# One activation table set, and the last row's inverse transform as four products without sums

## The reference

```python
x = x + attention(layernorm(x))               # 32 heads of 32, causal
x = x + autocorrelation(layernorm(x), ctx, ctx)
x = x + mix(layernorm(x))                     # four streams of 256
```

```python
corr = ifft(fft(q) * conj(fft(k))).real
w, idx = top_k(corr, 9); w = softmax(w)
out = sum_i w[i] * v[min(idx[i] + pos, L - 1)]
```

## Time and profile before

| what | value |
|---|---|
| median of 3 runs | 1248.21 us (1247.65 to 1251.31) |
| profiled execution, its own time | 1247.06 us |
| its span in the trace | 1245.1 us |
| PE busy | 1029.9 us, 83% |
| DVE busy | 932.4 us, 75% |
| ACT busy | 641.3 us, 52% |
| POOL busy | 492.4 us, 40% |

### The profile page before, as it was taken

The page is one execution under the profiler, slowest core; times in us unless marked ns, Lnnn a source line. Parts: engine busy times, 40 slices in busy tenths (PEclk is TensorE's granted clock), DMA queues, the critical chain, the costliest instruction groups (busy, mean ns, idle before and its releaser), DMA issues. The chain is left out here.

```text
span 1245.1 us, 23491 instructions
## 1 busy us (share of the span) xinstructions
PE 1029.9 (83%) x7928; PEld 781.0 (63%) x7928; DVE 932.4 (75%) x2818; ACT 641.3 (52%) x1827; POOL 492.4 (40%) x684
## 2 busy tenths in 40 slices
PE   5699999999999999999648999999887995615056
PEld 4577777787777777777436677767665663313034
DVE  6766787666678666666507778779998998897994
ACT  6434555544455544445516677778567655323133
POOL 2523443333343333344324666666565542201020
PEclk9799999999999999999679999999999997657578
DMA  9011011111101111110132123223222211139025
GB/s 377 25 42 57 19 57 57 57 57 40 45 28 57 57 57 57 40 41 19 58 120 85 68 83 117 89 77 123 73 81 81 73 39 38 43 120 332 0 56 131
DMA packets 47235, 95.72 MB, mean 77 GB/s; under 512 B 5952, under 2 KB 30400, under 8 KB 47168
## 3 DMA queue, kind: packets, MB, share of 16 engines
q1 hardware_dynamic: 47168, 94.91, 22.9%
HBM read 64.48 MB, written 27.26 MB: 74 GB/s over the span
## 5 line engine op out<-in xcount | busy, mean ns | idle before, releaser
L613 POOL TENSOR_TENSOR prob_G<-prob_G,rl 128x512 f32<-128x512 f32 x96 | 99.8, 1040 | 258.2 <-DVE rl L501 258.2
L383 ACT ACTIVATE prob_G<-prob_G,negm 128x128 f32<-128x128 f32 x384 | 148.8, 389 | 89.5 <-DVE negm L443 89.5
L244 PE MATMUL ps_qkv<-w_hi,xT_hi 128*128 128x512 f32 x384 | 156.7, 408 | 13.5 <-DVE prob_G L506 8.6
L245 PE MATMUL ps_qkv<-w_lo,xT_hi 128*128 128x512 f32 x384 | 151.4, 394 | 0.0
L246 PE MATMUL ps_qkv<-w_hi,xT_lo 128*128 128x512 f32 x384 | 151.2, 394 | 0.0
L316 PE MATMUL ps_qkv<-wo_hi,aT_hi 128*128 128x512 f32 x256 | 107.7, 421 | 0.0
L318 PE MATMUL ps_qkv<-wo_hi,aT_lo 128*128 128x512 f32 x256 | 102.1, 399 | 0.0
L317 PE MATMUL ps_qkv<-wo_lo,aT_hi 128*128 128x512 f32 x256 | 101.9, 398 | 0.0
L244 PEld LDWEIGHTS ps_qkv<-w_hi,xT_hi 128*128 128x128 f32 x384 | 73.2, 191 | 39.0 <-issue 16.1
L439 DVE TENSOR_TENSOR prob_G<-ps_s,mask 128x512 f32<-128x512 f32 x96 | 65.0, 677 | 41.4 <-PE ps_s L227 40.8
L468 DVE TENSOR_TENSOR xT_lo<-ps_t,xT_hi 128x512 fp32r<-128x512 f32 x16 | 11.1, 693 | 104.2 <-ACT xT_hi L422 104.2
(11 more groups left out here) (246 smaller groups left out, 2819.6 us busy)
## 6 DMA issues: line engine op xcount, KB each, us to landing
xin<-in_x SPq DMA_DIRECT2D x16, 512.0 KB, 3.3
xres<-in_x SPq DMA_DIRECT2D x16, 512.0 KB, 5.0
x<-xres SPq DMA_DIRECT2D x16, 512.0 KB, 2.6
c_xin<-x SPq DMA_DIRECT2D x16, 512.0 KB, 4.9
c_cin<-in_ctx SPq DMA_DIRECT2D x16, 512.0 KB, 4.2
c_b_xres<-x SPq DMA_DIRECT2D x16, 512.0 KB, 3.3
rows_x<-c_row SPq DMA_DIRECT2D x64, 128.0 KB, 2.3
m_xm<-rows_x SPq DMA_DIRECT2D x16, 512.0 KB, 8.6
```

What stands on the lines that cost most here:

```text
L244: nc.tensor.matmul(ps_qkv[:, n, :], xT_hi[:, k, :], w_hi[:, k, cols], start=k == 0, stop=False)
L245: nc.tensor.matmul(ps_qkv[:, n, :], xT_hi[:, k, :], w_lo[:, k, cols], start=False, stop=False)
L383: r = nc.scalar.activation(prob(g)[:, j, :], prob(g)[:, j, :], ACT.Exp, bias=negm[:, h:h + 1], accum_out=lsum[:, h:h + 1])
L613: nc.gpsimd.tensor_tensor(prob(g), prob(g), rl[:, g * GROUP:(g + 1) * GROUP].rearrange("p (j o) -> p j o", o=1).to_broadcast([P, GROUP, T] ...
```

## The change

Two edits. At ACT's start one set is named, which holds the logarithm beside the exponential and the copies, and is loaded there. In body 15 PE takes the four products themselves (the matrix that goes with each, `i % 2`, is that of the sum they belonged to), DVE makes the fourth with its sign turned, and POOL's sums of that body are gone. All bodies before it are as they were.

```diff
         @block.scalar
         def _(act):
+            nc.scalar.preload_act_table_set("natural_log_exp_and_others")
             act.wait_ge(const_in, 48)
...
                 def out_half(n):
+                    if not near:
+                        for i, part in enumerate((tw_re, tw_im, tw_re2, tw_im2)):
+                            if n == 0:
+                                pe.wait_ge(tw_done, 4 * b + (2, 2, 3, 4)[i])
+                            r = nc.tensor.matmul(p_b[:, n, :], mats[:, INV_OUT + i % 2, :], part[:, n * HALF:(n + 1) * HALF],
+                                                 start=i == 0, stop=i == 3)
+                        r.then_inc(out_ps, 1)
+                        return
...
-                        nc.vector.tensor_tensor(dst[:], src, of[:], ALU.mult).then_inc(tw_done, 1)
+                        if i == 3 and not near:
+                            nc.vector.scalar_tensor_tensor(dst[:], src, -1.0, of[:], ALU.mult, ALU.mult).then_inc(tw_done, 1)
+                        else:
+                            nc.vector.tensor_tensor(dst[:], src, of[:], ALU.mult).then_inc(tw_done, 1)
...
-                if far:
+                if far and near:
                     pool.wait_ge(tw_done, 4 * b + 3)
```

## The result

The changed kernel takes 1230.45 us, median of 4 runs (1229.03 to 1230.83). The kernel before took 1248.28 beside it, and the ratio is 0.985, 95% interval 0.9833 to 0.9868. Its profiled execution took 1230.26 with a span of 1228.4. The spans differ by 16.7; most of the rest of the 17.8 is that the execution profiled before was 1.2 faster than its own median, the changed one's only 0.2.

The account below looks back on a forecast made before the run. PE was taken as the bound up to body 7, DVE from body 8. Loads 8.9 plus body 15's 4.65 made 13.6 us: 1233.5 against the profiled 1247.06, 1234.6 for the median; range 1231 to 1242 for 8 in 10.

Parts of the forecast that it names:

- the term of 1.45: Body 6 into 7: without the load ahead of the exponential, the key spectrum PE waits for comes 1.45 us sooner.
- The first load of that turn: Body 6 into 7: this load delays only work that DVE doesn't yet need, so removing it gains 0.
- Start, 1.28: Kernel start: the load ahead of ACT's rounding of weights now runs while ACT waits for input, gaining 1.28 us.
- Body 11, body 14, body 17, the last exponential: Loads behind DVE's waits: body 11 gains 1.30 us, body 14 2.1, body 17 0.8, the end of mixing's chain_c 0.7.
- Body 15, 4.65: Body 15: DVE's 2.99 us wait for the second half goes, and 1.66 from chain steps slowed beside POOL's sums.
- The rival of the low clock: Body 15: PE's clock falls before the products, which take 1.91 us each; 6.2 us gained, 1242.0; 13%.
- The bounds of the fourth product: Body 15: the fourth product as scalar_tensor_tensor on DVE costs between 0 and +0.2 us more; 0 taken.
- The rule of half throughput: Body 15: by this rule the fourth product would take 1.1 us more, and the gain be 12.5 instead of 13.6.
- So all of it reaches the mixing phase: After body 15: bodies 16 and 17 take up none of the gain.
- Only the load at its end goes: 1.3: Mixing, chain_b: DVE's 9.1 us wait is mostly for rows read back; only its last load goes, 1.3 us.
- The drain: Rival at the loads: each also costs a drain, so 11 us more go and 1223.6 is left; 1%.
- two rivals: Low clock in body 15, 1242.0, 13%; gains before body 8 and in body 11 don't arrive, 1238.6, 17%.

Follow-up runs that it names:

- the set alone: The kernel before with only the one table set named at ACT's start, POOL's sums in body 15 kept: 1232.91 us.
- the products alone: The kernel before with only body 15's four products on PE without POOL's sums, all 25 loads kept: 1246.31 us.
- one moved line: chain_b's logarithms moved ahead of the take-outs of rows 0 and 1: on the changed kernel 1223.85 us; the same with POOL's sums in body 15 1230.24.

## Why the prediction was wrong

The direction, the places and most sizes held. The profiled execution was forecast at 1233.5 and took 1230.26: the sum failed by 3.2 us, of which the first point below is 1.8. The rest is the balance of small terms on both sides, some of them of single executions. Another 1.0 is the distance of the two profiled executions to their medians.

- **Body 6 into 7, the term of 1.45: the step that failed.** "PE stood idle 2.06 us for that spectrum. PE is the bound here: 1.45." The delay itself measured 1.62. But PE is the bound here, and its idle time was paid a second time in the work behind it, at half clock: 5.40 for the eight products instead of 3.70. The term measured 3.28. Both loads put back give exactly that, and with PE kept at work 1.85. I had the rule for body 15, where I priced the fall of the clock, and did not use it for the loads; the 5.40 stood in a row that I quoted.
- **The first load of that turn, priced at 0.** It holds back the squares, and so the second load. One load put back cost 0.79, both 3.28. They were one group, not one on the path and one hidden.
- **Start, 1.28.** It arrived (1.34 at DVE's first step behind it) and shrank to 0.5 by 820 in this trace. The low clock of 20.5 us near the end of the attention phase begins at 601.7 before and 601.5 after, so work that comes sooner can meet it at another place. How much is left is of the execution: -1.29 to +1.44 in twelve traces of the same program.
- **Body 11, body 14, body 17, the last exponential: 1.30, 2.1, 0.8, 0.7.** Measured 1.43, 2.26, 0.84 and 0.73. (Of the waits for the logarithms and exponentials there were seven and not six: DVE waits 0.5 for chain_c_logm too, before and after.)
- **959 to 1043 and the last rows, not priced: 1.09 and 0.73.** In the first the clock was low for 6.8 and 3.4 us before (ahead of the long low of body 14, which both have) and not at all after; in the last rows for 6.8 before and 3.4 after. The first can't be booked on the loads: the set alone gains 0.67 there, the products alone, with all their loads, 0.63, and both still have two low stretches of 3.4 us. So some 0.6 of the 1.09 is more likely what the profiled execution before had lost by itself. The second is firmer: of the eleven traces with the set named and nothing added at the last rows ten gain 0.73 to 0.87 there, and the products alone, with the load, gain 0.12; the pattern is that of body 7, and no experiment separates clock and load in it.
- **Body 15, 4.65.** Measured 4.77, and its two parts 3.05 and 1.72 where 2.99 and 1.66 were forecast. The rival of the low clock came in part: the clock fell after a wait of 1.23, and the slack of 1.4 took it up, with 0.56 of it left. The bounds of the fourth product, 0 to 0.2, held at 0. The rule of half throughput that I weighed against it (the Trainium skill, Vector Engine (DVE) Microarchitecture Reference, "7. Points that are easy to get wrong") is about two inputs in SBUF; this product has one of its two in the accumulators, so it doesn't test the rule: 1.22 either way. The row of 0.24 that has both the earlier trace rows is as fast as the plain form.
- **"So all of it reaches the mixing phase"** was right, and that the mixing phase would pass it on was not said but assumed. "Only the load at its end goes: 1.3" was 2.33 with the set alone and 0.32 with both. How long the wait is hangs on two rows' products, 1.97 or some 3.6 us each; in this trace both fell into the low clock, in three of four others with the same program from body 8 on only the first did.
- **The drain** (1%) is out: 1.29 to 1.30 from a load to the next start where one was put back. The range was too narrow below: nothing in it stood for a mechanism that makes loads dearer, though its upper end had two rivals.

Open: why the products alone lose another 2.60 up to 1223.4 (rows of the mixing phase at the low clock until 1202.1 there, until 1199.0 before, fit it; it wasn't tried), and what decides in which executions the clock falls in body 15 and at row 1. Each kernel has one trace, so how its other runs fell isn't known.

## What to carry to other kernels

Price a stall of PE twice: once as time, and once as the work behind it at half clock, read from the duration of that work against the same work elsewhere, and over more than one trace, since some falls come and go between executions. A gain passes through every long wait behind it, so before it is booked at the end, ask what ends that wait; if it stands in another engine's list behind work that isn't needed yet, moving it (here, by the medians, 6.6 us for one moved line with the four products and 2.7 with the sums) can be worth more than what was gained upstream (4.8 in body 15). Sums on POOL that stand beside DVE's two-input steps cost DVE time even when nobody waits for them.

## What the runs showed of the hardware that was not expected

Idle times of PE of 0.82 and 1.30 us left its clock up at one and the same place, 2.06, 2.07 and 2.09 didn't. In body 15, with the same instructions, idle times of 1.23, 1.28, 1.32, 1.47 and 1.47 us were followed by a fall and 0.80, 1.63 and 1.66 weren't, so there the length of the idle time alone doesn't decide. With sixteen matmuls that nothing needs PE's mean granted clock was 0.56 from 1098 to 1103 and 1.00 from 1103 to 1112, where the changed kernel's was 0.50 from 1108 to 1112. An unneeded sum on POOL made a DVE step of 128x128 take 0.81 instead of 0.29.
